# Macaron block on one core: the inverse deviation of the layer norms moves from ACT and DVE to POOL

## What is computed

```
def _layernorm(x, axis=-1, eps=1e-05):
    m = jnp.mean(x, axis=axis, keepdims=True)
    v = jnp.var(x, axis=axis, keepdims=True)
    return (x - m) / jnp.sqrt(v + eps)
...
    x = x + 0.5 * ffn(_layernorm(x), w1, w2, w3)      # norm 0, pass "ffn1"
    x = x + scan(_layernorm(x), W_x, W_dt, b_dt, A_log, D_param)   # norm 1
    x = x + 0.5 * ffn(_layernorm(x), w1, w2, w3)      # norm 2, pass "ffn2"
```

## Time and profile before

| | |
|---|---|
| timed runs | 922.63, 925.68, 927.62 us; median 925.68 us |
| span of the profiled execution | 922.9 us (its own time is given by the span alone) |
| granted PE clock, mean | 0.867 |
| DVE busy | 817.9 us, 89% |
| PE busy | 681.0 us, 74% |
| POOL busy | 591.3 us, 64% |
| ACT busy | 566.3 us, 61% |

### The profile page before, as it was taken

The page is one execution under the profiler, slowest core; times in us unless marked ns, Lnnn a source line. Parts: engine busy times, 40 slices in busy tenths (PEclk is TensorE's granted clock), DMA queues, the critical chain, the costliest instruction groups (busy, mean ns, idle before and its releaser), DMA issues. The chain is left out here.

```text
span 922.9 us, 15428 instructions
## 1 busy us (share of the span) xinstructions
PE 681.0 (74%) x5152; PEld 555.8 (60%) x5152; DVE 817.9 (89%) x1113; ACT 566.3 (61%) x1298; POOL 591.3 (64%) x418
## 2 busy tenths in 40 slices
PE   5566595368986888688986898789769894247568
PEld 4455374157865776567764786578557773035457
DVE  4974999899998999899989998999989998989931
ACT  5413565857587667955795768765885587355232
POOL 0370274776678758866777678876887488637502
PEclk7787797669997999889997998799979998559869
DMA  9300000000001000010001000100000000000000
GB/s 365 89 1 24 0 1 23 1 0 2 1 1 47 1 1 1 10 40 1 2 1 47 1 2 1 47 1 1 1 24 1 1 1 2 23 0 1 23 1 24
DMA packets 15009, 18.82 MB, mean 20 GB/s; under 512 B 3664, under 2 KB 12368, under 8 KB 14928
## 3 DMA queue, kind: packets, MB, share of 16 engines
q1 hardware_dynamic: 14928, 17.80, 5.6%
HBM read 13.60 MB, written 4.19 MB: 19 GB/s over the span
## 5 line engine op out<-in xcount | busy, mean ns | idle before, releaser
L344 PE MATMUL work<-x_hi,q 128*128 128x256 f16 x1408 | 338.0, 286 | 38.9 <-DVE hid L831 20.3
L344 PE MATMUL work<-x_lo,q 128*128 128x256 f16 x1408 | 336.7, 285 | 0.0
L1080 POOL TENSOR_TENSOR shared<-shared 128x1024 f32<-128x1024 f32 x120 | 284.5, 2371 | 60.3 <-DVE shared L902 59.9
L892 DVE TENSOR_TENSOR_SCAN shared<-decay,last_state,shared 128x256 f32<-128x256 f32 x448 | 304.4, 729 | 13.8 <-ACT decay L689 7.3
L689 ACT ACTIVATE decay<-shared,a_neg 128x256 f32<-128x256 f32 x512 | 221.1, 468 | 111.9 <-DVE shared L892 107.4
L1064 POOL TENSOR_TENSOR hid_lo<-hid,hid_hi 128x256 f16<-128x256 f32 x176 | 122.0, 707 | 137.9 <-ACT hid_hi L626 137.1
L344 PE MATMUL work<-hid_hi,q 128*128 128x256 f16 x704 | 162.6, 279 | 38.0 <-POOL hid_lo L1064 18.5
L344 PEld LDWEIGHTS work<-x_hi,q 128*128 128x128 f16 x1408 | 144.7, 103 | 71.8 <-DVE hid L831 25.7
L344 PE MATMUL work<-hid_lo,q 128*128 128x256 f16 x704 | 162.9, 279 | 0.0
L344 PEld LDWEIGHTS work<-x_lo,q 128*128 128x128 f16 x1408 | 144.3, 102 | 23.1
L879 DVE TENSOR_TENSOR shared<-shared,bc_row 128x1024 f32<-128x1024 f32 x128 | 154.9, 1210 | 0.3
(11 more groups left out here) (112 smaller groups left out, 788.2 us busy)
## 6 DMA issues: line engine op xcount, KB each, us to landing
x_in<-xT SPq DMA_DIRECT2D x8, 512.0 KB, 4.0
outT<-x SPq DMA_DIRECT2D x7, 512.0 KB, 3.2
shared<-w1T SPq DMA_DIRECT2D x4, 704.0 KB, 7.0
shared<-w2T SPq DMA_DIRECT2D x4, 704.0 KB, 11.5
shared<-w3T SPq DMA_DIRECT2D x3, 768.0 KB, 13.5
shared<-w3T SPq DMA_DIRECT2D x1, 512.0 KB, 15.2
outT<-x SPq DMA_DIRECT2D x2, 256.0 KB, 2.2
wx<-w_xT SPq DMA_DIRECT2D x1, 256.0 KB, 11.4
```

What stands on the lines that cost most here:

```text
L344: return nc.tensor.matmul(out, lhsT, rhs, start=start, stop=stop)
L892: nc.vector.tensor_tensor_scan(out=states[:, n % HR, k, :], data0=decay[pair][:, j, :], data1=dbx[:, n % 2, k, :], initial=state, op0=ALU. ...
L1080: nc.gpsimd.tensor_tensor(x2[:, par, :, :] if n == NS - 1 else y[:, 0, :, :], x1d[:, par, :, :] if n == 0 else y[:, 0, :, :], prod[:, n % ...
```

## The change

ACT writes the scaled variance plus epsilon (`var_eps`, `Identity` with the same scale and bias) where it wrote its square root. DVE's `invert_std` goes. POOL raises the 128x2 tile to the power -0.5, with a constant tile `neg_half` as the exponent. The semaphores keep their names (`ln2_std` now says that `var_eps` of norm 2 is written). ACT's, PE's and DVE's tables stay as they were but for the places of the reciprocals.

```
@@ tables
-    res2=[140, 151], centre2=22, recip2=53, norm2=60, centre1=73, recip1=92, norm1=93, centre0=133, recip0=143,
+    res2=[140, 151], centre2=22, norm2=60, centre1=73, norm1=93, centre0=133, 
...
-    fold_x0=60, x_lo0=141, bc_rest=120, add_x1=91)
+    fold_x0=60, x_lo0=141, bc_rest=120, add_x1=91, inverse2=40, inverse1=90)
@@ softplus_tail, in front of POOL's last operation
+            if before_u is not None:
+                before_u()
             engine.tensor_tensor(u[:, par, :, :], dt[:, par, :, :], xln[:, :, :], ALU.mult).then_inc(u_done, 1)
@@ ACT, ln_std_of
-                nc.scalar.activation(std[i][:, :], bank[:, 1, 0:TC // P], ACT.Sqrt, scale=s * s,
+                nc.scalar.activation(var_eps[i][:, :], bank[:, 1, 0:TC // P], ACT.Identity, scale=s * s,
                                      bias=zero_eps[:, e:e + 1]).then_inc(ln_std[i], 1)
@@ DVE (with its six calls)
-            def invert_std(i, count):
-                dve.wait_ge(ln_std[i], count)
-                nc.vector.reciprocal(rstd[i][:, :], std[i][:, :]).then_inc(ln_rstd[i], 1)
@@ POOL
+            def inverse_std(i, count):
+                pool.wait_ge(ln_std[i], count)
+                nc.gpsimd.tensor_tensor(rstd[i][:, :], var_eps[i][:, :], neg_half[:, :], ALU.pow).then_inc(ln_rstd[i], 1)
...
+            inverse_std(0, 1)
             ln_lo_of(0, 1, None)
...
             fold_squares(0, 2)
+            inverse_std(1, 1)
+            inverse_std(0, 2)
             ln_lo_of(0, 2, 0)
...
                     if now == AT_POOL["fold_sq2"]:
                         fold_squares(2, c)
+                    if now == AT_POOL["inverse2"]:
+                        inverse_std(2, c)
...
+                if not last(c) and now == AT_POOL["inverse1"]:
+                    inverse_std(1, c + 2)
...
-                    softplus_tail(pool, nc.gpsimd, c + 1, 1 - par)
+                    between = None if last(c) or before_last(c) else functools.partial(inverse_std, 0, c + 3)
+                    softplus_tail(pool, nc.gpsimd, c + 1, 1 - par, between)
...
             scan_all(pool, scan_chunk)
+            inverse_std(2, NC)
```

More of the change, by code:

```diff
@@ L11 @@
+import functools
 from contextlib import ExitStack
@@ L134, in macaron @@
         square = [sb(f"square{i}", [P, KD, TC]) for i in range(3)]
-        std = [sb(f"std{i}", [P, TC // P]) for i in range(3)]
+        var_eps = [sb(f"var_eps{i}", [P, TC // P]) for i in range(3)]
+        neg_half = sb("neg_half", [P, TC // P])
         rstd = [sb(f"rstd{i}", [P, TC // P]) for i in range(3)]
@@ L163, in macaron @@
         x2_free = [sem("x2_even_free"), sem("x2_odd_free")]
+        half_ready = sem("half_ready")
         consts_ready, sel_zeroed, sel_step = sem("consts_ready"), sem("sel_zeroed"), sem("sel_step")
@@ L253, in bcast, with softplus_tail @@
             return row.unsqueeze(1).to_broadcast([P, KD, TC])
-        def softplus_tail(waits, engine, c, par):
+        def softplus_tail(waits, engine, c, par, before_u=None):
             waits.wait_ge(sp_w, c + 1)
@@ L924, in _ @@
                                         apply_absolute_value=True).then_inc(abs_summed_dve, 1)
-            invert_std(0, 1)
             def quantise(m, piece, lo, hi):
@@ L965, in _ @@
             centre(0, 2, x_in[:, 1, :, :], ln0_bank)
-            invert_std(1, 1)
             normalise(1, 1, xln)
             make_first_x1d()
-            invert_std(0, 2)
             normalise(0, 2, centred[0], ln0_bank)
@@ L980, in beside_scan @@
                         centre(2, c, x2[:, 1 - par, :, :])
-                    if now == AT_DVE["recip2"]:
-                        invert_std(2, c)
                     if now == AT_DVE["norm2"]:
@@ L993, in beside_scan @@
                         centre(1, c + 2, x1[:, :, :])
-                    if now == AT_DVE["recip1"]:
-                        invert_std(1, c + 2)
                     if now == AT_DVE["bc_low"]:
@@ L1002, in beside_scan @@
                         centre(0, c + 3, x_in[:, par, :, :])
-                    if now == AT_DVE["recip0"]:
-                        invert_std(0, c + 3)
                     if now == AT_DVE["norm0"]:
@@ L1042, in _ @@
             fold(dve, nc.vector, fold_sq[2], NC, square[2], square[2])
-            invert_std(2, NC)
             normalise(2, NC, centred[2])
@@ L1095, in _ @@
                                     base=0, pattern=[[-1, P]], channel_multiplier=1).then_inc(ident_ready, 1)
+            nc.gpsimd.memset(neg_half[:, :], -0.5).then_inc(half_ready, 1)
+            pool.wait_ge(half_ready, 1)
             pool.sem_inc(fold_x[0], 2)
             pool.sem_inc(fold_sq[0], 2)
+            inverse_std(0, 1)
             ln_lo_of(0, 1, None)
```

## The result

| | before | after |
|---|---|---|
| median of the timed runs | 926.33 us (4 runs) | 960.62 us (4 runs, 959.57 to 961.87) |
| span of the profiled execution | 922.9 us | 957.8 us |
| granted PE clock, mean | 0.867 | 0.859 |

The changed kernel takes 1.0378 times as long, 95% interval 1.0355 to 1.0402. The forecast was 957.5 us, in a range of 938 to 976.

What follows compares the result with a forecast made beforehand. The prediction took DVE to bound the scan part. Norm 2 31.8, prologue 3.5 and end 0.4, less DVE's gain 3.9, made +31.8 us on 925.7 us: 957.5 us, range 938 to 976.

Steps and rivals of the forecast that it cites:

- Table loads gone: On ACT, 46 table loads go, 59 us, nearly all turning into longer idle time of ACT.
- DVE's gain of 3.9 us: On DVE, reciprocals removed from the scan part give 1.6 us and three waits for deviations 2.3 us.
- The power at p = 0.6 us: Assumed price p of one two-column POOL power, between bounds of 0.19 and 2.36 us.
- Norm 2, 6 x 5.3 = 31.8 us: Chunks 1 to 6: POOL waits for var_eps, delaying hid_lo, PE and normalise 3.3 us; PE's low clock adds 2.0 us.
- Norm 1 costs nothing up to p = 0.8: Loop's norm 1: power and spread finish in time; every tenth above p = 0.8 costs 0.1 us in 7 chunks.
- Norm 0 costs nothing: Loop's norm 0: POOL is free at 484.20 us, normalise comes 2.1 us later, leaving 1.3 us of slack.
- Prologue, +3.5 us: First norm 1: its power stands behind a fold, so normalise comes 3.5 us late and PE, ACT and DVE wait.
- End, +0.4 us: At the kernel's end the power replaces the reciprocal on the chain, 0.6 - 0.16 us.
- The wait without the clock: Rival, chance 0.25: norm 2's waits come but PE's clock holds, +19.8 us, 945.5 us.
- A slow power: Rival, chance 0.12: POOL's power takes p = 2 us, also delaying norms 1 and 0, +55.6 us, 981 us.
- Given back: Rival, chance 0.06: late engines find later waits shortened by as much; 0 to +4 us stay, 926 to 930 us.
- Faster: the freed ACT pays: Rival, chance 0.06: var_eps is ready when POOL comes, no norm waits, DVE saves waits on ACT: -14 us, 912 us.

Runs made afterwards that it cites:

- e3: The kernel before with ACT's Identity in place of Sqrt, so no table loads, wrong deviation value, all else kept: 924.82 us, ratio 0.9989.
- e4: The changed kernel with 42 more matmuls in PE's idle gap ahead of the last hid_lo wait, chunks 1 to 6, output not the reference's: 950.50 us.
- e1: The changed kernel with POOL's power of norm 2 at place 41, behind four hid_lo and add_y, instead of 40: 931.44 us.
- e8: The changed kernel with norm 2's power behind the four hid_lo but still ahead of add_y: 930.16 us.
- e7: e6 with DVE's normalise of norm 0 at place 151 instead of 150, behind one more pair of scans: 921.39 us.
- e10: The same kernel as e7 measured once more: 923.29 us.
- e6: e1 with the prologue's power of the first norm 1 moved ahead of the fold of norm 0's squares: 928.13 us.

## Why the prediction came out

The forecast was +31.8 us, the medians say +34.3 and the profiled spans +34.9. The mechanism of the largest term is right and tested. That the sum came so near is in part luck: norm 2 was taken too high by 2.2 us and the prologue by 2.3 (3.5 against the 1.2 at the start of the loop, of which 1.6 us come from this execution's early start), while norm 0 and the gates, at nothing in the sum, measured 4.6 and 2.2 us. By its own steps:

- **Table loads gone, worth nothing by themselves.** 59 us of ACT predicted, 60.0 measured, and e3 puts their worth at 0.6 us with an interval that includes zero. Right.
- **DVE's gain of 3.9 us.** The reciprocals gave 1.4 us of busy time for 1.6. The 2.3 us of waits for deviations are gone as a row. But 2.0 us of them (1.44 in chunk 0, 0.59 in chunk 2) stood at norm 0, where waits of 2.37 and 0.56 us for the spread stand now. So of this gain little is left, or, counted the other way, norm 0 costs some 2.5 us more than before and not 4.6.
- **The power at p = 0.6 us.** 24 instances took 695 to 721 ns. Right, within its bounds, and low by 0.1 us. The view of the power's line in the kernel after (shortest, median, longest in ns, first and last start in us):

```profile
L1048 POOL TENSOR_TENSOR rstd<-var_eps,neg_half x24: 695/700/721, 15.8 to 917.3; 128x2 f32<-128x2 f32 x24
```

- **Norm 2, 6 x 5.3 = 31.8 us.** The waits are 4.72, 5.20, 5.49, 4.01, 5.44 and 4.69 us, 29.6 in all. In chunk 3 step by step: from `var_eps` to the last `hid_lo` 3.3 us (3.2 predicted), from there to `normalise` 5.9 (5.7), and DVE wants it 3.7 us behind `var_eps` (3.6). The part without the clock, 3.3 us predicted, is 3.19 in e4; the clock's part, 2.0 predicted, is 10.4 / 6 = 1.7. Right in mechanism, and in size too, but the clock's share of it by two errors that cancel. I took 4.2 us of low clock from the earlier trace rows "after the restart", and the restart in the prediction is at 426.6 us, so that the clock would have been back at 430.8 and only some ten of the 24 matmuls slow, 1.1 us. I counted the 4.2 us from the end of the last `hid_lo` instead. In the kernel after the clock is low for 6.8 us, up to 446.2, and 22 of the 24 matmuls behind the last `hid_lo` run at it.
- **What else the gap in PE does.** Not in the sum: DVE's waits for gates grew from 6.6 to 8.8 us. They grew by nearly as much in e1 (8.7) and e8 (8.4), where no `normalise` of norm 2 waits, and in e4 (8.1), where the clock stays up, so the clock isn't their cause. In e7 and e10, where no product of norm 0 waits, they are back at 6.9 and 6.8; so they seem to go with norm 0, by which step I did not follow.
- **Norm 1 costs nothing up to p = 0.8.** With p = 0.70 no `normalise` of norm 1 in the loop waits. Right.
- **Norm 0 costs nothing.** This is the step that failed: 4.6 us of waits in six chunks. I counted from POOL, free at 484.20 us, and called it the later of the two events. The later one is `var_eps`, behind PE's variance. These rows of the kernel before, from the timelines of PE, ACT and DVE in chunk 3, were there to be read:

```profile
482.60 1.95 PE L344 MATMUL stat<-mean_w,square 128*128 128x1 f32 x16 [1.51 <-ACT square L596]
```
```profile
484.62 0.26 ACT L603 ACTIVATE std<-stat,zero_eps 128x2 f32<-128x2 f32 x1
```
```profile
486.41 1.19 DVE L819 TENSOR_TENSOR centred<-centred,stat 128x1024 f32<-128x1024 f32 x1
```

  The variance ends at 484.55. `var_eps` (0.26), power (0.70) and spread (0.75) then reach 486.3, and DVE is ready for the product at 486.33. The prediction's slack of 1.3 us is the room that it gave to the power, of which 0.7 us would have been left at p = 0.6. Counted from `var_eps` the room is 0.70 us, all of it taken by the power. e7 shows it from the other side: with `normalise` one scan pair later all these waits are gone. I had read POOL's and DVE's rows, and not PE's and ACT's.
- **Prologue, +3.5 us.** From DVE's subtraction of the mean ahead of it (80.44 us before, 78.85 after) to `xln` it is 2.96 us before and 6.53 after, 3.6 us more, and e6 gets 3.0 us of it back. Right for `xln`. In the profiled execution 2.0 us of it show there, for the reason above, and 1.2 us at the start of the loop, since waits behind `xln` became shorter. That not all of it reaches the loop was not in the sum.
- **End, +0.4 us.** From the last fold to the product 3.30 us before, 3.89 after: +0.6.

**Rivals.** "The wait without the clock" at 945.5 us is e4, 950.5: its term was right (19.1 us for 19.8), and what it lacks are norm 0 and the gates. "A slow power" fell with p = 0.70 us. "Given back" fell: DVE's waits for decays and for means together are 12.2 us before and after (7.3 + 4.9 and 9.2 + 3.0), so nothing of the stalls came back there. "Faster: the freed ACT pays" is the instructive one. It did not happen in this kernel, since POOL's wait at place 40 hangs on a scan, as predicted. With three pieces moved (e7, e10) the kernel is 0.3 to 0.4% faster than before, but not by DVE's waits on ACT: its idle time is 31.7 us for 32.1, and its busy time is 2.1 us (e7) and 2.7 us (e10) shorter. What the freed ACT gives there is a place for norm 0 that costs the kernel before 4.3 us.

## What to carry to other kernels

When work moves to another engine, price the place first and the instruction second: a 0.7 us power cost 29 us because it waited ahead of four `hid_lo` that PE needed sooner, and behind those four it cost none of the 29. For each place take the *latest* of all inputs (the queue's own engine, the producer, the producer's producer), from rows of each of them; the one step that failed here took one of three. Time freed on an engine that nobody waits for is worth nothing until another piece is moved to use it: the loads were worth 0 in one order of the work, and in another the kernel with them was 7.5 us slower than the one without loads and reciprocals, 4.5 us of it in DVE's waits.

## What was unexpected in the hardware's rows

- In chunk 3 the clock reads 1.00 for most of PE's 4.99 us of idle time and falls only some 0.2 us before its end. Most of the low stretch (439.4 to 446.2, at 0.50) lies behind the gap, with PE at work again.
- A POOL power of 128x2 takes 0.70 us with a spread of 26 ns over 24 instances, about that of a 128x256 add (0.73 us).
- Two executions of one kernel (e7, e10) differ by 1.94 us at the first `xln` and by 2.0 us in span, with waits in the loop alike to 0.1 us.
